# Mixing the experts' rows at the end of a two-layer language-model tower: where the row buffers lie, and where in the order the chunks are mixed

## The reference

```
out = h + sum over 8 experts e of comb[:, e] * swiglu(x, Wg[e], Wu[e], Wd[e])  +  swiglu(x, sg, su, sd)
swiglu(x, g, u, d) = (silu(x @ g.T) * (x @ u.T)) @ d.T          hidden width 384, all float32
```

## Time and profile before

| what | us |
|---|---|
| median of three runs | 1852.68 |
| the three runs | 1856.21, 1852.68, 1847.51 |
| the profiled execution | 1844.46 |
| its span, first to last instruction | 1842.8 |

### The profile page before, as it was taken

One profiled execution on the slowest core, in us unless ns is written; L12 is line 12 of the kernel. 1 busy time (PEld: TensorE's weight loads), 2 busy tenths in 40 slices (PEclk: granted clock), 3 DMA queues, 4 the chain that ended last, 5 costly groups with the idle time before them and its releaser, 6 DMA issues. The chain is left out here.

```text
span 1842.8 us, 28573 instructions
## 1 busy us (share of the span) xinstructions
PE 1604.2 (87%) x8964; PEld 868.2 (47%) x8965; DVE 1090.2 (59%) x2488; ACT 628.0 (34%) x849; POOL 423.5 (23%) x518
## 2 busy tenths in 40 slices
PE   5769999999899999674999917999988989999995
PEld 3421332233233232473566604667775646666653
DVE  5858998899799892365333326564624933333336
ACT  3411666566566668210111102212123112222110
POOL 6540000000000000101555514000000226666630
PEclk9855999999999999875999967999888879999998
DMA  2481222022222200720111122000002301111125
GB/s 82 148 139 16 34 32 39 2 35 34 35 35 35 35 1 1 194 83 7 35 43 41 38 61 66 2 18 10 18 10 70 102 18 51 53 51 53 47 56 185
DMA packets 64848, 92.83 MB, mean 50 GB/s; under 512 B 9905, under 2 KB 50036, under 8 KB 63732
## 3 DMA queue, kind: packets, MB, share of 16 engines
q1 hardware_dynamic: 51520, 65.08, 15.9%
q0 software_dynamic: 12288, 25.18, 4.6%
q10 hardware_dynamic: 960, 1.57, 0.6%
HBM read 61.82 MB, written 29.98 MB: 50 GB/s over the span
## 5 line engine op out<-in xcount | busy, mean ns | idle before, releaser
L507 DVE TENSOR_REDUCE sa_half_max<-psum 128x1 f32<-128x512 f32 x768 | 494.4, 687 | 75.7 <-PE psum L610 55.9
L564 ACT ACTIVATE sa_probs<-psum 128x1024 f32<-128x1024 f32 x384 | 372.3, 1022 | 167.9 <-PE psum L601 166.3
L610 PE MATMUL psum<-k_stack,q_stack 96*128 96x512 bf16 x768 | 285.6, 410 | 26.7 <-PEq L401 14.9
L601 PE MATMUL psum<-q_stack,k_stack 97*128 97x512 bf16 x768 | 231.1, 385 | 6.2 <-ACT sa_probs L564 5.4
L610 PEld LDWEIGHTS psum<-k_stack,q_stack 96*128 96x128 bf16 x768 | 75.0, 98 | 281.4 <-issue 148.1
L633 PE MATMUL psum<-sa_probs,sa_v_ext 128*32 128x512 f32 x1536 | 206.4, 609 | 0.6 <-ACT sa_probs L564 0.6
L1555 PE MATMUL psum<-w_e_up_a,ex_xt 128*128 x448 | 172.0, 527 | 0.0
L1419 ACT ACTIVATE ex_silu<-psum 128x384 f32<-128x384 f32 (+1 forms) x112 | 59.3, 529 | 290.0 <-PE psum L1555 287.4
L1571 PE MATMUL psum<-w_e_down,ex_g_t 128*128 x752 | 137.2, 334 | 0.5 <-DVE ex_g_t L1451 0.5
L1571 PEld LDWEIGHTS psum<-w_e_down,ex_g_t 128*128 128x128 f32 x752 | 120.7, 190 | 34.4 <-issue 34.4
L1459 DVE COPY ex_to_rows<-slot_rows 128x2 uint32 (+1 forms) x56 | 10.4, 185 | 212.0 <-DMA y_rows<-ex_y,ex_to_rows 121.7
(11 more groups left out here) (282 smaller groups left out, 2207.4 us busy)
## 6 DMA issues: line engine op xcount, KB each, us to landing
q_stack<-qk_parts SPq DMA_DIRECT2D x66, 128.0 KB, 4.6
k_stack<-qk_parts SPq DMA_DIRECT2D x66, 128.0 KB, 7.6
qk_parts<-ep_parts SPq DMA_DIRECT2D x16, 384.0 KB, 3.2
x_tokens<-x SPq DMA_DIRECT2D x16, 384.0 KB, 2.6
ex_rows<-y_rows SPq DMA_DIRECT2D x16, 384.0 KB, 4.6
qk_parts<-ep_parts SPq DMA_DIRECT2D x16, 192.0 KB, 4.1
w_e_down<-e_down SPq DMA_DIRECT2D x1, 3072.0 KB, 33.1
attn<-y_rows SPq DMA_DIRECT2D x8, 384.0 KB, 3.4
```

The source lines that it names most:

```text
L507: nc.vector.tensor_reduce(half_max[:, g, hd, qt, half:half + 1], slot, AX.X, ALU.max).then_inc(ring_free[r], 1)
L564: nc.scalar.activation(probs[:, st % 2, 2 * pair:2 * pair + 2, :], ps[:, 2 * pair:2 * pair + 2, :], ACT.Exp, scale=SCALE0).then_inc(exp_do ...
L601: last = nc.tensor.matmul(ps[:, hd, :], kst[:, g, hd, kt * P:(kt + 1) * P], qst[:, g, hd, half * HALF:(half + 1) * HALF], start=True, stop ...
L610: last = nc.tensor.matmul(ps[:, 4 + r, :], qst[0:SK, g, hd, qt * P:(qt + 1) * P], kst[0:SK, g, hd, half * 512:(half + 1) * 512], start=Tru ...
```

## The change

Three things are changed in `experts`, for the second layer alone. The tile `rows` is no longer allocated; the row buffers, four instead of two, lie in `attn`, which they fill (4 buffers x 2 rows x 4 tiles = 32 tiles), and two more semaphores `landed` go with them. SP issues loads 0 to 3, then load c and store c - 4 in turn for c = 4 to 7, then the last four stores. VectorE mixes one chunk behind each product from the third one on (behind products 17 to 23, chunks 0 to 6), behind the adds where there are any; chunk 7 and the last adds come at the end.

```diff
         if layer == 1:
 
-            BUFS = 2
-            rows = sb("rows", [P, BUFS, k_top, CT, D])
+            BUFS = 4
+            rows = s.attn[:].rearrange("p (b k j) d -> p b k j d", b=BUFS, k=k_top)
             landed = [new_sem(f"ex_landed{p}") for p in range(BUFS)]
...
                 for c in range(BUFS):
                     load(c)
-                for c in range(CHUNKS):
+                for c in range(BUFS, CHUNKS):
+                    load(c)
+                    store(c - BUFS)
+                for c in range(CHUNKS - BUFS, CHUNKS):
                     store(c)
-                    if c + BUFS < CHUNKS:
-                        load(c + BUFS)
                 sp.wait_ge(out_stored, START + 16 * CHUNKS)
...
             chunks_mixed = 0
+            FIRST_MIX = 2
             for n in behind:
                 shared_product(nc, dve, s, n)
                 chunk, f = divmod(n, SharedExpert.PARTS)
                 if f == 0 and chunk > SHARED_AHEAD:
                     shared_add(nc, dve, s, chunk - 1)
-                    until = min(CHUNKS, 2 * (chunk - SHARED_AHEAD))
-                    for c in range(chunks_mixed, until):
-                        mix(c)
-                    chunks_mixed = until
+                if n - behind[0] >= FIRST_MIX and chunks_mixed < CHUNKS - 1:
+                    mix(chunks_mixed)
+                    chunks_mixed += 1
             if layer == 1:
                 for c in range(chunks_mixed, CHUNKS):
                     mix(c)
```

## The result

The changed kernel takes 1834.09 us (median of eight runs, 1831.71 to 1841.41); the kernel before, in eight runs with the three shown above among them, 1847.37 us (1843.82 to 1856.21). The ratio is 0.9928, with an interval from 0.9905 to 0.9951. The profiled execution took 1832.01 us, with a span of 1830.3.

What follows compares the result with a forecast made beforehand. VectorE's row mixing, with waits for loads, bounds the tail after TensorE ends; 11.3 us gained less 0.1 for semaphores gives 11.2, so 1852.68 becomes 1841.5 us; range from 6 us below that to 1848.5.

Steps and rivals of the forecast that it cites:

- The sum for the tail: VectorE's new order written out by hand: last add starts at 1825.95 instead of 1837.24, 11.3 us earlier.
- VectorE caught up at product 21: After starting 2.1 us late, VectorE finishes chunk 3 at 1810.95, before product 21 is ready at 1811.24.
- two chunks and one add left: Behind product 23 only chunks 6 and 7 and the last add remain, the add at 1825.95.
- TensorE's two stalls gone: TensorE's two waits of 0.17 us for late products, at 1806.24 and 1819.47, were to disappear.
- The term for two semaphores: Between routing and experts, SP sets up two more semaphores; cost between nothing and 0.26 us, taken as 0.1.
- The rows' place in `attn`: VectorE's mixing reads rows from new memory; no price taken, or end 0.2 us later if chunks always took 2.85.
- Its tightest slack is 1.5 us: Least spare time in the written order: product 18 ends 1.54 us before TensorE takes it at 1801.89.
- free up to a landing at 1798.44: Chunk 0's rows may land until 1798.44 at no cost; beyond that the full lateness is paid.
- Eight issues last until 1796.4: SP issues the eight transfers of loads 0 to 3 at 0.51 us each, with nothing else standing on SP then.
- The eight loads are served in turns: Rival, 8%: queued transfers share engines evenly, load 0 lands at 1805.2; gain 4.4 us, time 1848.3.
- The change does not do all that it says: Rival, 7%: VectorE does not catch up, one more chunk stays behind the last product; gain 8.4 us, time 1844.3.
- The clock rival: Rival, 3%: TensorE's 6.76 us wait for product 18 drops its clock; 20 us more if it stays down, 1868 us.

Runs made afterwards that it cites:

- before_again: The kernel before, unchanged, run again for a second profile; tail (product 15 start to last add start) 50.29 us, product 15 starting at 1794.08.
- before_third: The kernel before, unchanged, run for a third profile; tail (product 15 start to last add start) 50.49 us, product 15 starting at 1795.57.
- order_alone: Changed kernel with the two old row buffers in their old tile, so only the new order stays; tail 41.37 us, ratio to the kernel before 0.9947.
- after_again: The changed kernel run again without an edit; tail 39.12 us, 1834.58 us, ratio to the kernel before 0.9945.
- buffers_alone: Changed kernel with four buffers but VectorE's old mixing order; tail 44.89 us, ratio to the kernel before 0.9979.
- late_load: Changed kernel, SP issuing the first loads only when product 17 is done; tail 41.12 us against 39.12 in the changed kernel, not timed.
- first_mix_0: Changed kernel with the first chunk mixed behind product 15 instead of 17; tail 44.39 us against 39.12, one execution, not timed.
- first_mix_1: Changed kernel with the first chunk mixed behind product 16 instead of 17; tail 41.98 us against 39.12, one execution, not timed.
- act_scales: Changed kernel, ScalarE multiplying rows of chunks 4, 5 and 6 by their weights, VectorE only adding them; tail 36.41 us, ratios to the kernel before 0.9927 and 0.9920.

## Why the prediction was right about the tail and missed the time

**What held.** The sum for the tail came out: 11.3 us worked out, 11.29 measured. So did its parts: the chunk at 2.76 in a row of work, the product at 0.69, chunk 0 with one wait for its load and a product late behind it, VectorE caught up at product 21, two chunks and one add left, TensorE's two stalls gone. That the sum came out to 0.01 us is partly luck: chunk 0 waited 1.65 us instead of 2.1, and this error left no trace because VectorE waits for product 21 in either case (0.83 us here, 0.29 in the written order). The term for two semaphores (0.1) is 0.12 by the rows that answer to the earlier trace rows:

```profile
1479.76 0.20 DVE L1273 CAST slot_tokens<-ro_slot_row 128x72 uint32<-128x72 f32 x1
1482.39 0.18 POOL L1336 COPY ex_tokens<-slot_tokens 128x2 uint32<-128x2 uint32 x1 [12.52 <-POOLq L1316]
```

From start to start that gap is 2.63 us, 2.51 before. It is 2.51 or 2.52 in before_again, before_third and order_alone too, which do without the two semaphores, and 2.62 or 2.63 in after_again, buffers_alone, late_load, first_mix_0 and first_mix_1, which have them. The rows' place in `attn` has no price: 5.61 us for 16 instructions there, 5.60 in the old tile.

**The step that failed** is "The median of the three runs shown is 1852.68 ... less 11.2 gives 1841.5", and with it the range "from 6 us below the forecast". I had the 8.2 us between that median and the profiled execution in hand and took three runs for the level of the kernel. It was 5 to 7 us too high: the same kernel has medians of 1847.37 in eight runs with those three, 1846.01 in 23 and 1846.19 in 11. From 1847.37 the same sum gives 1836.2, and from 1846.0 it gives 1834.8, with 1834.09 and 1834.58 measured beside them. What is left, 2.1 and 0.2 us, is within what medians of the same code differ by here: the two of act_scales, 1835.12 and 1831.88, lie 3.2 apart. The rows say why three runs are a poor level: the part ahead of the tail differs by up to 15 us between executions of the same code. The range did not hold its own reason either: "a set of runs as low as the profiled one" lies 8.2 us below the forecast, at 1833.3, and not 6, and with 8.2 it would have taken in both measured medians. The median of all four executions in hand, the profiled one among them, is 1850.1; from it the same sum and the same 6 us would have reached down to 1832.9.

**Smaller errors that cost nothing here.** "Its tightest slack is 1.5 us": it is 1.11, because TensorE's first matmul down of a chunk also waits for the adds behind product 18; late_load shows that wait by name. By the times of the prediction itself it was 0.6 (the adds end at 1801.29, TensorE wants them at 1801.89), so "free up to a landing at 1798.44" should have read 0.9 us earlier, and the price of a late load 0 was some 0.9 us too small. The diff does not touch `shared_down`, and I did not follow its waits. "Eight issues last until 1796.4": they take 7.3 us instead of 4.1, with nothing waiting for them. The second transfer of load 1 took 6.9 us to land (6.2 in the earlier trace rows); it landed at 1799.0 and chunk 1 started at 1799.48, so that was close to becoming a wait.

**The rivals.** "The eight loads are served in turns" did not come: load 0 landed 4.2 us behind its second issue, as with four in the queue, and the others behind it (in first_mix_1 that landing took 5.6). "The change does not do all that it says" did not come either. The clock rival was right in kind and wrong in its two sizes: the clock fell behind a wait of 3.84 us already, and it cost 1.7 to 2.1 us, not 20, because it came back while TensorE worked. This is also what the Trainium skill, TensorE: Matmul & The Clock Gate, states in Part 1 (activity lifts the throttle), and these two runs agree with it. With a price like that it could not have turned the sign: 6.8 + 0.9 + 2.1 = 9.8 us, an estimate from these runs, is still less than 11.2.

## What to carry to other kernels

When an engine off the bound has its work in a lump behind the last stage, writing out its order by hand, with the durations of its own rows, gives the gain to a few tenths of a microsecond; for every slack follow all waits of the instruction that uses the result, those in functions the change leaves alone too. Forecast a time from a level that many runs support, or as a difference, and read the scatter ahead of the changed stage before giving a range. Work is best moved to an engine whose instructions leave those of the busy engine at their length: here ScalarE took part of the mixing for nothing, and POOL gave back all that it took.

## What the runs showed of the hardware

SP's issues were slower when many of its transfers were under way (issued and not yet landed). In the changed kernel's tail every issue that started with up to four transfers under way took 0.36 to 0.51 us; with five or six under way 12 of 13 took 0.71 to 1.91 us (the other 0.36). The sixth, seventh and eighth took 1.09, 1.58 and 1.91 us, and they ended 0.3, 0.8 and 0.8 us behind the landings of the first three transfers, while the transfer engines moved some 320 to 370 GB/s. The number alone does not settle it, since in the kernel before some issues with two to four under way took 0.74 to 0.89 us; why the queue stalls was not tried. The clock of TensorE can fall after its wait is over: in first_mix_1 it was at 1.00 through the whole wait, fell within the second stretch of work behind it (0.65) and stood at 0.50 in the third.
